# Count matrix of a graph: source one-hots of four columns in one vector operation, read against a row of numbers in PSUM

## The chip, the cores and the metric

The kernel runs on one core of one Trainium2 chip. The metric is the device time of one execution in microseconds (us), lower is better. A core has five engines that run their own instruction streams and meet at semaphores: PE (TensorE, matmuls; its weight loads are shown as PEld), DVE (VectorE), ACT (ScalarE), POOL (GpSimd) and SP (SyncE). Here POOL issues the indirect DMAs (gathers), and SP hands out buffers.

## What is computed

Four graph layers run one after the other on 6250 nodes of 128 features, with 106250 edges `src -> dst` and a 128-wide attribute per edge:

```python
x = layernorm(x + L0(x, src, dst))            # mean over in-neighbours
x = layernorm(x + L1(x, edge_attr, src, dst)) # H[head]@Wa + E@Wb, summed both ways over all edges
x = layernorm(x + L2(x, src, dst))            # two attention convolutions
x = layernorm(x + L3(x, src, dst))            # four mean aggregations, top k between them
```

The kernel turns `segment_sum(x[src], dst)` into dense matmuls with a count matrix `A[src, dst]` (how many edges lead from src to dst). Layer 1 also needs, per source node, the sum of the attributes of its edges. The change lies in the part that makes `A` and these sums.

## The kernel before, in words

Nodes are padded to NP = 6272 in NT = 49 tiles of P = 128. Part a sorts the edges by source into a list `listed` of COLS = 896 columns by 128 partitions; each entry has the edge's number, its destination and its source. Part b, which the change touches, loads the list as `entry`, and turns the sources and destinations into f32 (`key_id`, `key_dst`) and the sources into int16 as well (`key_src`).

**The matrix.** For each of 49 source tiles ("lines") and each of 7 windows of WIDE = 896 destinations there is a cell. A cell is a loop (`cell`, once on PE, once on DVE) whose turns take four columns of the list each. In a turn DVE makes for each of the four columns a one-hot of the source within the tile, 128 wide (L1009: compare the int16 row `iota` with the key of the partition), and a one-hot of the destination in the window, 896 wide (L1011). PE multiplies them (L823, two matmuls of 448 columns for each list column, eight a turn) into one of three PSUM buffers of two banks (`ps_cell`, banks 0 to 5). ACT copies a full buffer to `line` (L890), clears it (L880) and writes each line to `adjacency` in HBM. The one-hots stand in `hot`, a ring of two turns, each in two halves of two columns: `s_hot` tells PE that a half is written, `s_hot_free` tells DVE that PE has read one. Before each half DVE waits for the same half of the turn before last.

**The sums.** POOL gathers attribute rows of the list, eight columns to a unit and UNITS = 112 units, one indirect DMA for each column (L804), into `row_ring`, which holds four units. SP goes through the units in order: it waits until PE has summed unit u (L779, `s_sum`, a `hold` whose line is L69), gives its place free (L780, `s_unit_free`), and then waits for the four semaphores of the next unit of that place (L771) before it tells PE of it (L772, `s_rows`) and turns to unit u + 1. PE makes the sums in 81 steps of two (`two`, L832 to L844): each takes two pairs (tile, unit), for each of them eight f32 matmuls (L841) of the source one-hots `is_src` with the rows, into `ps_row`, banks 6 and 7. DVE adds a sum to `edges_out` (`add`, L1031) and makes the `is_src` of the step after next (`hot_of`, L1024, 128 x 1024 f32 out of two int16 tables in SBUF).

**The order** is written out by hand and the same on PE and DVE. PE: `two(i)`, cells 4 to 6 of line s, `two(i + 1)`, cells 0 to 3 of line s + 1. DVE: cells 4 to 6 of line s, `turned_over(i)`, cells 0 to 3 of line s + 1, `turned_over(i + 1)`. Each sixth line has no step of two (`TURN`). `hold` (L67 to L69) is a wait with an increment of a semaphore that nobody reads. `bc` is a broadcast by stride 0.

```python
for half in range(2):                                             # DVE, cell(), L1005
    hold(dve, s_hot_free, turn * 2 + (half + 1), s_held_dve)
    for j in range(2): ...                                        # L1009, L1011 for column 2 * half + j
for h in range(2):                                                # DVE, turned_over(), L1036
    add(i, h, pair[h]); hot_of(parity, h, later[h])
```

## Time and profile before

| what | value |
|---|---|
| median of 3 runs (lowest, highest) | 8150.13 us (8149.39, 8155.3) |
| the profiled execution, its span | 8157.6 us, 8155.7 us |
| PE, DVE, ACT, POOL busy over the span | 73%, 53%, 27%, 43% |
| part b, first to last matmul of the matrix | 1276 to 2803 us of the span |

The profiled execution is 7.5 us above the median of the runs; its span leaves out 1.9 us around the first and the last instruction. The profile gives for each group of instructions the line, the engine, how often it ran, the busy time, the mean of one, and the idle time of the engine before it with what ended that idle time. Such a wait is put down to the instruction whose semaphore came last. "issue" is idle time that no semaphore ended: the engine's own sequencer was still at loop, register and wait instructions, which are not counted as busy.

### The profile page before, as it was taken

The numbers are of one execution on the slowest core, as the hardware profiler recorded it, in microseconds if no ns is written. First come the engines' busy times: TensorE is split into PE (matmuls) and PEld (weight loads), VectorE is DVE, ScalarE is ACT, GpSimd is POOL, SyncE is SP. The second block draws the span as 40 slices with busy tenths as digits, with TensorE's granted clock in tenths as the row PEclk, the third lists the DMA queues.
The fourth block names the chain that finished last, engine by engine and source line by source line (L and its number), as shares of the span: only waits on it lengthen the run. The fifth ranks groups of instructions, "written<-read, shape, count | busy, mean of one in ns | idle before, by whom it ended". The sixth has DMA issues, their size and how long they took to land. (4 is left out here: it accounts for less than half of the span.)

```text
span 8155.7 us, 149095 instructions
## 1 busy us (share of the span) xinstructions
PE 5989.6 (73%) x38791; PEld 4139.6 (51%) x38792; DVE 4345.4 (53%) x11705; ACT 2230.5 (27%) x4994; POOL 3467.9 (43%) x3568
## 2 busy tenths in 40 slices
PE   0366625666666599999976777767777769996899
PEld 0255523334443255555546766757666635553555
DVE  9677737667776412222227777767777730103311
ACT  1011203434443300100004555535555500000200
POOL 4777766666665100000007777747777600000400
PEclk9987768999999899999988999989999989997999
DMA  0122212222223356777752222212222246663566
GB/s 18 43 71 69 71 38 79 91 98 96 92 96 95 79 169 171 180 188 179 191 125 57 54 55 56 54 48 54 55 55 55 47 129 188 191 198 113 146 195 178
DMA packets 835186, 849.24 MB, mean 104 GB/s; under 512 B 417947, under 2 KB 779130, under 8 KB 828347
## 3 DMA queue, kind: packets, MB, share of 16 engines
q1 hardware_dynamic: 710381, 560.82, 25.2%
q0 software_dynamic: 115904, 201.65, 10.9%
q10 hardware_dynamic: 8464, 81.36, 2.5%
q8 instruction: 222, 3.64, 0.2%
q14 instruction: 215, 1.76, 0.1%
HBM read 665.89 MB, written 97.31 MB: 94 GB/s over the span
## 5 line engine op out<-in xcount | busy, mean ns | idle before, releaser
L1954 POOL DMA_INDIRECT d_row_ring<-table_att,src_at x1664 | 1579.2, 949 | 639.0 <-issue 486.4
L2576 PE MATMUL psum<-e_a_ring,e_parts 128*128 128x448 bf16 x6174 | 1184.8, 353 | 75.9 <-DVE e_parts L2690 75.9
L804 POOL DMA_INDIRECT b_row_ring<-edge_attr,b_entry x896 | 902.4, 1007 | 565.3 <-SPq L780 325.2
L823 PE MATMUL psum<-b_hot 128*128 x2872 | 660.9, 367 | 462.4 <-DVE b_hot L1011 276.1
L363 POOL DMA_INDIRECT listed<-a_record,a_slot_no x832 | 811.8, 976 | 338.8 <-issue 271.9
L2576 PEld LDWEIGHTS psum<-e_a_ring,e_parts 128*128 128x128 bf16 x6174 | 605.1, 98 | 632.4 <-issue 81.0
L1363 PE MATMUL psum<-c_a_ring,c_parts 128*128 128x448 bf16 x4116 | 812.8, 356 | 45.4 <-DMA c_a_ring<-adjacency 40.7
L1979 PE MATMUL psum<-edges_out,edges_in 128*128 128x120 f32 x4896 | 678.2, 297 | 160.3 <-ACT edges_in L2045 159.3
L1979 PEld LDWEIGHTS psum<-edges_out,edges_in 128*128 128x128 f32 x4896 | 628.5, 208 | 205.7 <-issue 205.7
L823 PEld LDWEIGHTS psum<-b_hot 128*128 x2872 | 282.9, 98 | 820.7 <-issue 719.1
L1011 DVE TENSOR_SCALAR b_hot<-b_iota,b_key_dst 128x896 int16 x1436 | 690.1, 481 | 4.9 <-issue 4.6
L1995 PE MATMUL psum<-edges_out,edges_in 128*128 128x132 f32 x4896 | 651.5, 288 | 16.7 <-DVE edges_out L2217 15.9
L1009 DVE TENSOR_SCALAR b_hot<-b_iota,b_key_id (+1 forms) x1436 | 386.9, 269 | 450.3 <-PE psum L823 388.0
L1277 POOL DMA_DIRECT2D table_att<-c_h_row x21 | 15.7, 746 | 1431.6 <-DVEq L1701 1431.6
L1995 PEld LDWEIGHTS psum<-edges_out,edges_in 128*128 128x128 f32 x4896 | 598.0, 197 | 38.7 <-DVE edges_out L2217 23.7
L1363 PEld LDWEIGHTS psum<-c_a_ring,c_parts 128*128 128x128 bf16 x4116 | 404.4, 99 | 418.0 <-DMA c_a_ring<-adjacency 50.6
L890 ACT CAST b_line<-psum 128x896 f32 x343 | 310.4, 905 | 905.4 <-PE psum L823 871.9
L841 PE MATMUL psum<-b_row_ring,b_is_src 128*128 x2592 | 348.8, 295 | 218.7 <-SPq L772 143.4
L405 PE MATMUL psum<-a_later 128*128 x2432 | 418.5, 342 | 55.4 <-ACT a_later L448 55.0
L841 PEld LDWEIGHTS psum<-b_row_ring,b_is_src 128*128 128x128 f32 x2592 | 326.8, 206 | 257.8 <-issue 257.6
L405 PEld LDWEIGHTS psum<-a_later 128*128 128x128 f32 x2432 | 392.1, 251 | 128.2 <-issue 127.1
L2167 DVE TENSOR_TENSOR edges_in<-psum,edges_out 128x1024 bf16<-128x1024 f32 x306 | 374.7, 1224 | 106.3 <-issue 60.7
(477 smaller groups left out, 8043.1 us busy)
## 6 DMA issues: line engine op xcount, KB each, us to landing
e_a_ring<-adjacency SPq DMA_DIRECT2D x1029, 224.0 KB, 2.8
c_a_ring<-adjacency SPq DMA_DIRECT2D x686, 224.0 KB, 2.9
adjacency<-b_line ACTq DMA_DIRECT2D x49, 1568.0 KB
a_later<-edge_attr SPq DMA_DIRECT2D x103, 512.0 KB
d_row_ring<-table_att,src_at POOLq DMA_INDIRECT x1664
b_row_ring<-edge_attr,b_entry POOLq DMA_INDIRECT x896
listed<-a_record,a_slot_no POOLq DMA_INDIRECT x832
e_a_left<-adjacency_left SPq DMA_DIRECT2D x28, 224.0 KB, 3.3
```

Of the source, the lines that this page charges most:

```text
L363: pool.indirect_dma_start(out=listed, out_offset=bass.IndirectOffsetOnAxis(ap=slot_no[:, c:c + 1], axis=0), in_=record[:, c, :], in_offset ...
L405: mm = nc.tensor.matmul(ps_in[h], is_dst[:, h, c, :], row_ring[:, unit, c, :].rearrange("p a f -> p (a f)"), start=(c == 0), stop=(c == G ...
L804: pool.indirect_dma_start(out=row_ring[:, u % 4, g, 0:D], out_offset=None, in_=a["edge_attr_128"], in_offset=bass.IndirectOffsetOnAxis(ap= ...
L823: mm = nc.tensor.matmul(ps[:, v, :], four[:, half, j, 0:P], four[:, half, j, P + v * WIN:P + (v + 1) * WIN], start=False, stop=True, skip_ ...
L841: mm = nc.tensor.matmul(ps_row[h], is_src[:, parity, h, c, :], row_ring[:, bass.ds(unit & 3, 1), c, :].rearrange("p a f -> p (a f)"), star ...
L1009: V.tensor_scalar(four[:, half, j, 0:P], iota[:, bass.ds(tile * P, P)], ids[:, c:c + 1], None, ALU.is_equal)
L1011: last = V.tensor_scalar(four[:, half, j, P:], iota[:, window], ends_at[:, c:c + 1], None, ALU.is_equal)
L1363: mm = nc.tensor.matmul(psum[:, b + v, 0:WIN], parts[:, piece, tile, :], rows[:, v * WIN:(v + 1) * WIN], start=(s == 0 and piece == 0), st ...
L1954: pool.indirect_dma_start(out=row_ring[:, u % 4, g, :], out_offset=None, in_=table_att[layer], in_offset=bass.IndirectOffsetOnAxis(ap=src_ ...
L1979: mm = nc.tensor.matmul(psum[:, 3 + h, c * SLOTS:(c + AGAIN) * SLOTS], is_dst[:, h, c, :], bc(ranked[:, h, c, :], 1, [P, AGAIN, SLOTS]), s ...
L1995: mm = nc.tensor.matmul(ps_out, is_dst[:, h, c, :], weighted[:, c, :], start=(c == 0), stop=(c == G - 1))
L2576: mm = nc.tensor.matmul(psum[:, 2 * (turn % 2) + v, 0:WIN], (few_parts if d == 2 else parts)[:, piece, s, :], a_ring[:, (FIRST[turn] + s) ...
```

## The change

- `hot`'s four source one-hots of a turn are made by one DVE operation on 128 x 4 x 128 elements in place of four on 128 x 128: (key - first node of the tile) == position, with `key_id` broadcast along the 128 positions, the tile's first node as a scalar per partition out of the new table `tile_at` (made by one more iota on POOL), and the positions 0 to 127 out of `ps_iota`, a row of 128 f32 in PSUM bank 7, written once.
- `is_src` is made by the same kind of operation on 128 x 8 x 128, in place of a comparison of two int16 tables. `key_src` and the operation that fills it go.
- DVE waits once a turn, for both halves of the turn before last. `s_hot` is still told twice a turn, after the destinations of columns 0 and 1, and of 2 and 3.
- Both sums of a step lie in bank 6. PE therefore waits for both adds of the step before at the head of `two`, and DVE waits for both sums before its first add; `turned_over` makes both adds first and then both one-hots.

```diff
--- before.py
+++ after.py
@@ -132,7 +132,6 @@
         columns = sb("columns", [P, NT])
         tables = sb("tables", [P, 2 * COLS + COLS // 2 + P * QJ + UNITS + 1])
         column_key = tables[:, 0:COLS]
-        key_src = tables[:, 2 * COLS:2 * COLS + COLS // 2].bitcast(I16)
         out_pairs = tables[:, 2 * COLS + COLS // 2:2 * COLS + COLS // 2 + P * QJ].bitcast(I32)
         out_end = tables[:, 2 * COLS + COLS // 2 + P * QJ:].bitcast(I32)
         rank_peak = sb("rank_peak", [P, 1], I32)
@@ -680,6 +679,7 @@
             key_dst = sbb("key_dst", [P, COLS])
             reach = sbb("reach", [P, 2, COLS])
             hit = sbb("hit", [P, COLS])
+            tile_at = sbb("tile_at", [P, NT + 1])
             cell_no = sbb("cell_no", [P, CI])
             cell_f = sbb("cell_f", [P, 4, CI])
             cell_i = sbb("cell_i", [P, 2, CI], I32)
@@ -722,7 +722,8 @@
             s_left_out = bsem("s_left_out")
 
             ps_cell = [psum[:, 2 * k:2 * k + 2, 0:WIN] for k in range(3)]
-            ps_row = [psum[:, 6 + k, 0:D + 1] for k in range(2)]
+            ps_row = [psum[:, 6, h * (D + 1):(h + 1) * (D + 1)] for h in range(2)]
+            ps_iota = psum[:, 7, 0:P]
             buffer_of = [w % 3 for w in range(NWIDE)]
             last_use = [max(v for v in range(w - NWIDE, w) if buffer_of[v % NWIDE] == buffer_of[w]) for w in range(NWIDE)]
 
@@ -783,6 +784,7 @@
             @blk.gpsimd
             def _(pool):
                 nc.gpsimd.iota(iota[:], [[1, NP + P]], base=0, channel_multiplier=0)
+                nc.gpsimd.iota(tile_at[:], [[P, NT + 1]], base=0, channel_multiplier=0, allow_small_or_imprecise_dtypes=True)
                 nc.gpsimd.iota(cell_no[:], [[1, CI]], base=0, channel_multiplier=CI, allow_small_or_imprecise_dtypes=True)
                 nc.gpsimd.iota(cell_real[:], [[1, CI]], base=0, channel_multiplier=CI)
                 nc.gpsimd.iota(count_up[:, 0, :], [[-1, COLS]], base=COLS, channel_multiplier=0,
@@ -833,10 +835,10 @@
                         cell(ps_cell[buffer_of[w]], n, at0)
 
                 def two(i, parity, pair):
+                    pe.wait_ge(s_added, i * 2 + 2)
                     for h, (_, unit) in enumerate(pair):
                         hold(pe, s_rows, unit + 1, s_held_pe)
                         pe.wait_ge(s_is_src, i * 2 + (h + 1))
-                        pe.wait_ge(s_added, i * 2 + (h + 1))
                         for c in range(G):
                             mm = nc.tensor.matmul(ps_row[h], is_src[:, parity, h, c, :],
                                                   row_ring[:, bass.ds(unit & 3, 1), c, :].rearrange("p a f -> p (a f)"),
@@ -919,7 +921,6 @@
                 V = nc.vector
                 dve.wait_ge(s_entry, 16)
                 st.by(V.tensor_copy(key_id[:], entry[:, :, 2]))
-                st.by(V.tensor_copy(key_src, entry[:, :, 2]))
                 st.by(V.tensor_copy(key_dst[:], entry[:, :, 1]))
                 st.settle(dve)
                 st.by(V.tensor_copy(reach[:, 0, :], key_dst[:]))
@@ -990,6 +991,8 @@
                 st.by(V.tensor_tensor(cell_row[0:1, 1, :], cell_row[0:1, 1, :], cell_row[0:1, 0, :], ALU.bitwise_or))
                 st.settle(dve)
                 dve.wait_ge(s_table, 1)
+                st.by(V.tensor_copy(ps_iota, iota[:, 0:P]))
+                st.settle(dve)
                 dve.sem_inc(s_table, 1)
                 dve.sem_inc(s_hot_free, HOT)
                 dve.sem_inc(s_added, 2)
@@ -999,16 +1002,15 @@
                     with dve.Fori(0, n) as g:
                         k = nc.s_assert_within(dve.snap(k0 + g * 4), 0, COLS - 4,
                                                skip_runtime_bounds_check_because="k0 is at most COLS - 4 n")
-                        ids, ends_at = key_id[:, bass.ds(k, 4)], key_dst[:, bass.ds(k, 4)]
+                        ends_at = key_dst[:, bass.ds(k, 4)]
                         turn = dve.snap(at0 + g)
-                        four = hot[:, bass.ds(turn & 1, 1), :, :, :].rearrange("p a h j f -> p (a h) j f")
+                        four = hot[:, bass.ds(turn & 1, 1), :, :, :].rearrange("p a h j f -> p (a h j) f")
+                        hold(dve, s_hot_free, turn * 2 + 2, s_held_dve)
+                        V.scalar_tensor_tensor(four[:, :, 0:P], bc(key_id[:, bass.ds(k, 4)], 2, [P, 4, P]),
+                                               tile_at[:, bass.ds(tile, 1)], bc(ps_iota, 1, [P, 4, P]), ALU.subtract, ALU.is_equal)
                         for half in range(2):
-                            hold(dve, s_hot_free, turn * 2 + (half + 1), s_held_dve)
-                            for j in range(2):
-                                c = 2 * half + j
-                                V.tensor_scalar(four[:, half, j, 0:P], iota[:, bass.ds(tile * P, P)],
-                                                ids[:, c:c + 1], None, ALU.is_equal)
-                                last = V.tensor_scalar(four[:, half, j, P:], iota[:, window],
+                            for c in (2 * half, 2 * half + 1):
+                                last = V.tensor_scalar(four[:, c, P:], iota[:, window],
                                                        ends_at[:, c:c + 1], None, ALU.is_equal)
                             last.then_inc(s_hot, 1)
 
@@ -1021,12 +1023,13 @@
 
                 def hot_of(parity, h, code):
                     tile, unit = code
-                    V.tensor_tensor(is_src[:, parity, h, :, :], bc(key_src[:, bass.ds(unit * G, G)], 2, [P, G, P]),
-                                    bc(iota[:, bass.ds(tile * P, P)], 1, [P, G, P]), ALU.is_equal).then_inc(s_is_src, 1)
+                    V.scalar_tensor_tensor(is_src[:, parity, h, :, :], bc(key_id[:, bass.ds(unit * G, G)], 2, [P, G, P]),
+                                           tile_at[:, bass.ds(tile, 1)], bc(ps_iota, 1, [P, G, P]), ALU.subtract, ALU.is_equal
+                                           ).then_inc(s_is_src, 1)
 
                 def add(i, h, code):
                     at = bass.ds(code[0], 1)
-                    dve.wait_ge(s_sum, i * 2 + (h + 1))
+                    dve.wait_ge(s_sum, i * 2 + 2)
                     hold(dve, s_added, i * 2 + (h + 2), s_held_dve)
                     V.tensor_tensor(edges_out[:, at, :].rearrange("p a f -> p (a f)"),
                                     edges_out[:, at, :].rearrange("p a f -> p (a f)"), ps_row[h], ALU.add
@@ -1035,6 +1038,7 @@
                 def turned_over(i, parity, pair, later):
                     for h in range(2):
                         add(i, h, pair[h])
+                    for h in range(2):
                         hot_of(parity, h, later[h])
 
                 for i in range(2):
```

In DVE's loop of a cell (L1009, now L1009, the sources; L1011, now L1013, the destinations; ISA, REGISTER_ALU and the like are the sequencer's own). Before:

```order
L1009 ISA
L1009 TENSOR_SCALAR b_hot<-b_iota,b_key_id 128x128
L1011 ISA
L1011 TENSOR_SCALAR b_hot<-b_iota,b_key_dst 128x896
L67 REGISTER_ALU
L1009 ISA [waits b_s_hot_free]
L1009 TENSOR_SCALAR b_hot<-b_iota,b_key_id 128x128
L1011 ISA
L1011 TENSOR_SCALAR b_hot<-b_iota,b_key_dst 128x896
```

Now:

```order
L1009 REGISTER_ALU [waits b_s_hot_free]
L1009 ISA
L1009 REGISTER_ALU
L1009 ISA
L1009 SCALAR_TENSOR_TENSOR b_hot<-b_key_id,b_tile_at,psum 128x4x128
L1013 ISA
L1013 TENSOR_SCALAR b_hot<-b_iota,b_key_dst 128x896
```

A turn had eight DVE operations in alternation and a second wait in its middle; it now has one operation on the sources, then the four on the destinations, and the wait stands ahead of all five.

In DVE's `turned_over`, the first pair of a step (L1031, now L1034: the add; L1024, now L1026: the one-hots of the sources). Before:

```order
L67 REGISTER_ALU [waits b_s_sum]
L1031 REGISTER_ALU [waits b_s_added]
L1031 REGISTER_ALU
L1031 ISA
L1031 TENSOR_TENSOR edges_out<-edges_out,psum 128x129
L1024 REGISTER_ALU
L1024 ISA
L1024 REGISTER_ALU
L1024 ISA
L1024 TENSOR_TENSOR b_is_src<-tables,b_iota 128x1024
```

Now:

```order
L1034 TENSOR_TENSOR edges_out<-edges_out,psum 128x129
L67 REGISTER_ALU [waits b_s_sum]
L1034 REGISTER_ALU [waits b_s_added]
L1034 REGISTER_ALU
L1034 ISA
L1034 TENSOR_TENSOR edges_out<-edges_out,psum 128x129
L1026 REGISTER_ALU
L1026 ISA
L1026 REGISTER_ALU
L1026 ISA
L1026 SCALAR_TENSOR_TENSOR b_is_src<-b_key_id,b_tile_at,psum 128x1024
```

The second add moved ahead of the first one-hots.

On PE, the head of `two` (L838 and L841 before, L838 to L843 now). Before:

```order
L67 REGISTER_ALU
L67 ISA
L838 ISA [waits b_s_rows]
L841 REGISTER_ALU [waits b_s_added,b_s_is_src]
L841 ISA
L841 MATMUL psum<-b_row_ring,b_is_src 128x129
```

Now:

```order
L838 ISA
L67 REGISTER_ALU [waits b_s_added]
L67 ISA
L841 REGISTER_ALU [waits b_s_rows]
L843 REGISTER_ALU [waits b_s_is_src]
L843 ISA
L843 MATMUL psum<-b_row_ring,b_is_src 128x129
```

The wait for the adds moved ahead of the wait for the rows, and is made once for both pairs.

## Rows read from the trace of the kernel before

**Rows 1.** Groups of instructions by line, stretch 1276 to 2803 us (columns as first line)

```profile
line engine op names shapes xcount | busy us, mean ns | idle before us <-releasers
L804 POOL DMA_INDIRECT b_row_ring<-edge_attr,b_entry x867 | 865.5, 998 | 556.5 <-SPq L780 325.2 <-issue 231.3
L823 PE MATMUL psum<-b_hot 128*128 x2872 | 660.9, 367 | 462.4 <-DVE b_hot L1011 276.1 <-issue 164.7 <-ACT b_line L890 12.3
L841 PE MATMUL psum<-b_row_ring,b_is_src 128*128 x2592 | 348.8, 295 | 218.7 <-SPq L772 143.4 <-issue 60.1 <-DVE b_is_src L1024 11.1
L1024 DVE TENSOR_TENSOR b_is_src<-tables,b_iota 128x1024 f32 x160 | 195.5, 1222 | 8.6 <-issue 4.9
```

**Rows 2.** Waits, 1276 to 2803 us: who, for whom, us, times, longest us

```profile
DVE b_hot L1009 <- PE psum L823: 388.0, 161, 19.0
```

**Rows 3.** Waits of SP's queue, 1276 to 2803 us

```profile
SPq L771 <- DMA b_row_ring<-edge_attr,b_entry: 1352.4, 109, 18.5
SPq L69 <- PE psum L841: 24.6, 4, 7.8
```

**Rows 4.** Timeline, DVE and PE, 2035 to 2043 us: start us, us, engine, line

```profile
2035.01 1.74 PE L823 MATMUL psum<-b_hot 128*128 x8 [0.97 <-issue]
...
2037.05 0.25 DVE L1009 TENSOR_SCALAR b_hot<-b_iota,b_key_id  x1 [0.77 <-PE psum L823]
2037.22 0.45 DVE L1011 TENSOR_SCALAR b_hot<-b_iota,b_key_dst 128x896 int16 x1
2037.58 0.25 DVE L1009 TENSOR_SCALAR b_hot<-b_iota,b_key_id  x1
2037.68 1.82 PE L823 MATMUL psum<-b_hot 128*128 x8 [0.94 <-issue]
...
2040.01 0.25 DVE L1009 TENSOR_SCALAR b_hot<-b_iota,b_key_id  x1 [0.77 <-PE psum L823]
...
2040.47 1.77 PE L823 MATMUL psum<-b_hot 128*128 x8 [0.97 <-issue]
```

**Rows 5.** Timeline of PE, 1808 to 1834 us, a stretch of lines without a step of two

```profile
1811.57 1.75 PE L823 MATMUL psum<-b_hot 128*128 x8 [0.96 <-DVE b_hot L1011]
1816.66 8.04 PE L823 MATMUL psum<-b_hot 128*128 x24 [3.35 <-DVE b_hot L1011]
```

**Rows 6.** Timeline, a `turned_over` of DVE and the gathers of POOL under it

```profile
2023.97 0.94 POOL L804 DMA_INDIRECT b_row_ring<-edge_attr,b_entry  x1 [0.30 <-issue]
...
2024.32 0.28 DVE L1031 TENSOR_TENSOR edges_out<-edges_out,psum 128x129 f32 x1
2024.65 1.23 DVE L1024 TENSOR_TENSOR b_is_src<-tables,b_iota 128x1024 f32 x1
...
2025.22 1.47 POOL L804 DMA_INDIRECT b_row_ring<-edge_attr,b_entry  x1 [0.30 <-issue]
...
2027.13 0.25 DVE L1009 TENSOR_SCALAR b_hot<-b_iota,b_key_id  x1
```

**Rows 7.** Timeline of POOL, first and last of 46 long gathers under L1024

```profile
1325.20 1.83 POOL L804 DMA_INDIRECT b_row_ring<-edge_attr,b_entry  x1 [2.10 <-SPq L780]
...
2636.80 1.48 POOL L804 DMA_INDIRECT b_row_ring<-edge_attr,b_entry  x1 [6.19 <-SPq L780]
```

**Rows 8.** Instructions on tiles and lines: duration ns min/median/max, first and last start us

```profile
L804 POOL DMA_INDIRECT b_row_ring<-edge_attr,b_entry x896: 938/944/2454, 1229.5 to 2696.1; - x180
...
L2167 DVE TENSOR_TENSOR edges_in<-psum,edges_out x306: 1224/1224/1226, 4299.5 to 6505.0; 128x1024 bf16<-128x1024 f32 x153
...
L2217 DVE TENSOR_TENSOR edges_out<-d_row_ring,psum x306: 1247/1254/1256, 4318.2 to 6521.2; 128x1056 f32<-128x1056 f32 x153
```

**Rows 9.** The page's groups: the gathers of the attention layer

```profile
L1954 POOL DMA_INDIRECT d_row_ring<-table_att,src_at x1664 | 1579.2, 949 | 639.0 <-issue 486.4
```

**Rows 10.** Durations of two operations of the new kind (columns as rows 8)

```profile
L950 DVE SCALAR_TENSOR_TENSOR b_hit<-b_reach,b_cell_no,b_line x8: 1152/1152/1152, 1237.7 to 1253.9; 128x896 f32<-128x896 f32 x8
...
L2703 DVE SCALAR_TENSOR_TENSOR e_y<-psum,col_w_deg,e_r_b_s x98: 340/343/352, 6674.9 to 7459.2; 128x128 f32<-128x128 f32 x98
```

**Rows 11.** Timeline, the start of part b

```profile
1208.75 0.55 POOL L786 IOTA b_cell_no<- 128x4 f32 x1
...
1263.62 0.41 DVE L981 CAST b_hit<-b_cell_row 1x512 f32<-1x512 int32 x1 [4.93 <-DMA b_cell_row<-cell_rows]
```

## The prediction

> **What bounds the kernel now.** Only part b changes, 1527 us of the 8155.7 us span, so the question is what those 1527 us wait for. I read first the groups of that stretch, to see which engine is full. None is: the matmuls of the matrix and of the sums take 661 + 349 us of PE [rows 1]. So I read what PE's idle time ends with, and then the timeline of single turns.
>
> PE's turn. In a stretch with nothing but cells, PE starts a turn at 2035.01, 2037.68 and 2040.47 us, every 2.7 us; 1.8 us of it are the eight matmuls, and 0.94 to 0.97 us are idle with "issue" behind them, the loop's own registers [rows 4]. There are 2872 / 8 = 359 turns: 359 x 2.7 = 969 us. The 276 us that the groups put down to DVE are for the most part this same 0.95 us, and once, before the first turn, the start of the part. A step of two sums has 2592 / 81 = 32 matmul records, 349 / 81 = 4.3 us, and (218.7 - 143.4) / 81 = 0.9 us of idle time of its own [rows 1]: 81 x 5.2 = 421 us. That makes 1390 us of work that PE's instruction stream needs whatever the others do. The rest is one wait: 143.4 us for SP L772, the attribute rows [rows 1]. 1390 + 143 = 1533, against 1527.
>
> The row stream. SP spent 1352.4 us waiting for gathered rows, and 24.6 us, four times, waiting for PE [rows 3]. It frees a place only after the unit before has landed, so POOL never has more than one unit to fetch: eight gathers of 998 ns with 0.3 us between them, then 325.2 / 108 = 3.0 us until the next place is free [rows 1]. It is a serial chain over the whole part, nearly never held up by PE, and PE waits on it 143 us. **So the rows bound part b first, PE's own stream second; DVE is third:** it waits 388 us for PE to free one-hots [rows 2].
>
> **Part by part.**
>
> 1. *Four source one-hots in one operation.* Old: from L1009's start to L1011's is 0.17 us, from L1011's to the next L1009 0.36 us [rows 4]; a turn is 4 x 0.53 = 2.1 us, plus 0.77 us of idle time before the next turn, 2.96 us from 2037.05 to 2040.01. New operation, from its kind [rows 10]: 1152 ns for 896 elements and 343 for 128 give 1.053 ns an element and 208 ns fixed, so 512 elements last 747 ns; less the 0.08 us by which the next operation starts before the end (0.25 long, next after 0.17) that is 0.67 us, against 4 x 0.17 = 0.68. DVE's data time stays. What falls is its instruction stream: three operations with their register instruction and one wait fewer a turn. The turn can become anything from 2.1 us (the 0.77 all hidden) to 2.96 (nothing); I take 2.3, since five instructions of 0.67 and 0.36 us give the sequencer time that eight of 0.26 on average do not. By itself it earns nothing, because DVE is not the bound; see 4.
>
> 2. *One wait a turn, for both halves.* From PE's freeing to the first half ready was 0.77 + 0.17 + 0.36 + 0.17 + 0.45 = 1.9 us and becomes 0.77 + 0.67 + 0.36 + 0.45 = 2.25 us. `hot` holds two turns, so PE works 2.7 us on the other one meanwhile. Cost nothing; the cover is PE's turn, 0.45 us of it are left. Behind the wait stand this turn's five operations and, after a line's part, the adds, for which nobody is in haste, as PE needs them a step later.
>
> 3. *`is_src` out of one SBUF table and PSUM.* The operation gets longer, 208 + 1024 x 1.053 = 1286 ns against 1222: 162 x 0.06 = 10 us of DVE, hidden by its 388 us of waiting. What it does to POOL is the main term. A gather lasts 944 ns in the median [rows 8] but 998 in the mean [rows 1]: 867 x 54 = 47 us too long. Under L1024 a gather took 1.47 us, just before it 0.94 [rows 6]. 46 gathers of over 1.23 us overlap an L1024, the first and the last are shown [rows 7], together 32 us over the median, and all gathers that overlap one have 36 us of the 47. L1024 reads two SBUF tables. Where DVE instead reads one SBUF tensor and PSUM, in the attention layer, L2167 and L2217 run 306 x 2.5 = 760 us [rows 8] beside 1664 gathers whose mean is 949 [rows 9]. So the 36 us should go. Bounds: 0, if the new operation stops gathers as the old did, and 47. They are taken off a serial chain; PE's 143 us of row waits are there to be shortened by them. About a tenth of the units are fetched while it is PE that is late (SP's waits, three of them inside the part [rows 3]), so -33 us.
> The Trainium skill says otherwise here ("SBUF — State Buffer", Who interferes with whom): vector operations with two SBUF inputs disturb only GpSimd instructions that read SBUF, a `tensor_tensor` was seen not to stall a gather's descriptors, and it is `tensor_scalar` in its two-port modes that does. The trace has it the other way round, 1.47 us under L1024 against 0.94 under L1009 and L1011. By the page the sum would lose nearly all of this term; that is rival B.
>
> 4. *A faster DVE turn where DVE does set the pace.* On lines without a step of two, PE does seven and more cells in a row and DVE's 2.96 us are longer than PE's 2.7. There PE's idle time before a turn is 3.35 us instead of 0.96 [rows 5], 2.4 us too long, once in each of the eight blocks of six lines: 19 us. After most of them PE runs into a wait for rows anyway, which takes it back. Three of SP's waits for PE follow such a stretch, and after the last one no rows are waited for: 4 x 2.4 = -9 us. Bounds 0 and -19.
>
> 5. *Order of adds and the waits for them.* PE waits 11.1 us before L841 for L1024 [rows 1], which I read as the second add standing behind it. Now both adds come first. The same cells lie between as before, so no wait is added; what goes is mostly followed by a wait for rows. 0 (bounds -11, 0). DVE's wait for both sums: PE made them three cells earlier. 0.
>
> 6. *The start.* One more small iota on POOL, 0.55 us by its nearest row; the copy to PSUM, 0.41 by a copy of 512 [rows 11]; four longer `is_src`, 0.24; the first half 0.34 later (2.). The copy to `key_src` goes, beside POOL's iotas: nothing. +1.4 us.
>
> Sum: -33 - 9 + 1.4 = -41 us. The profiled execution, 8157.6 us, would become 8117; from the median of the runs, 7.5 us lower, 8150.1 - 41 = **8109 us**.
>
> **The rivals.** A difference under 0.2% (16 us) can't be told from none.
>
> A, the forecast: gathers freed of L1024. With the bounds of 3, 4 and 5: from -47 - 19 + 1 = -65 (8085) to -24 + 1 (8127) where a third of the gathers' 36 us stays and term 4 earns nothing.
>
> B, *the gathers stay as slow as they are*. Then only the share of the four small L1009 a turn goes. Outside L1024 the excess is 47 - 36 = 11 us, and L1009 has 0.17 of every 0.53 us: -3.5. With 4 and 6: -3.5 - 9 + 1.4 = -11, 8139 us, no difference. For it speaks the skill's rule above; against it rows 6 and 9.
>
> C, *slower: DVE becomes the bound*. If the new operation takes two cycles an element, it needs 0.53 us more, a turn is 2.96 + 0.53 = 3.5 us if the idle 0.77 us also stay, and a `turned_over`, 2.8 us now (2024.32 to 2027.13 [rows 6]), takes 2 x 1.07 more: 359 x 3.5 + 81 x 4.95 = 1657 us, 130 more than the 1527: 8280 us. The point from which it decides is a turn of (1527 - 401) / 359 = 3.1 us, 0.18 above today's. Answer time would be 2.8 us, over PE's 2.7. Against it stands row L950, two f32 SBUF sources and 1152 ns for 896 elements. The skill's "Vector Engine (DVE) Microarchitecture Reference", Points that are easy to get wrong, says that this shape with two non-bf16 SBUF sources has half the throughput; L950 doesn't show it, and here one source is in PSUM.
>
> D, more than forecast: terms 3, 4 and 5 all at their far bounds and PE's steps shorter besides, -47 - 19 - 11 + 1 = -76: below 8085.
>
> **How the numbers follow.** A 0.72, B 0.17, C 0.05, D 0.06. Faster: A and D, 0.78. Same: B, 0.17. Slower: C, 0.05. The range leaves out C and D and takes in B's price with a few us for the spread of the runs: 8085 to 8145; A's own range is 8085 to 8127.
>
> **What would show it.** The mean of the gathers near 955 ns (B: 990 and more); the `is_src` operation near 1290 ns and the new `hot` one near 750 (C: 1280); PE's wait for SP about 105 us instead of 143; DVE's idle time before its turns longer, its turn 2.3 us where it is not held; no 3.35 us before PE's turns. The forecast is wrong if gathers get faster and PE's wait for rows does not fall, for then the rows were not the chain that I take them for, and wrong in its second term if PE still stands before single turns for DVE, which would say that the answer time of 2. is longer than reckoned.

## The result and the profile after

The changed kernel takes 8168.2 us (median of 14 runs, 8159.7 to 8181.6) against 8150.9 (14 runs of the kernel before on the same chip; one of them took 20795 us and is left out of the ratio): ratio 1.0022, 95% interval 1.0015 to 1.0029, **slower by 17 us**. The forecast was 8109, 41 us faster. In two more comparisons the changed kernel was slower by 13.2 and 17.6 us; on average 16.

The groups of part b of the changed kernel (columns as in [rows 1]; L806 are the gathers, L825 and L843 PE's matmuls of the matrix and of the sums, L1009 the new operation for four source one-hots, L1013 the destinations, L1026 `is_src`, L1034 the adds):

```profile
L806 POOL DMA_INDIRECT b_row_ring<-edge_attr,b_entry x864 | 865.2, 1001 | 560.4 <-SPq L781 329.9 <-issue 230.4
L825 PE MATMUL psum<-b_hot 128*128 x2872 | 666.9, 372 | 452.9 <-DVE b_hot L1013 369.3 <-issue 75.4 <-ACT b_line L892 7.0
L1013 DVE TENSOR_SCALAR b_hot<-b_iota,b_key_dst 128x896 int16 x1435 | 561.2, 454 | 0.0
L843 PE MATMUL psum<-b_row_ring,b_is_src 128*128 x2592 | 353.5, 298 | 221.9 <-SPq L773 146.3 <-DVE b_is_src L1026 45.3 <-issue 29.9
L1009 DVE SCALAR_TENSOR_TENSOR b_hot<-b_key_id,b_tile_at,psum 128x512 f32 x358 | 266.8, 745 | 457.1 <-PE psum L825 387.1 <-issue 69.6
L1026 DVE SCALAR_TENSOR_TENSOR b_is_src<-b_key_id,b_tile_at,psum 128x1024 f32<-128x1024 f32 x160 | 197.8, 1278 | 11.1
L1034 DVE TENSOR_TENSOR edges_out<-edges_out,psum 128x129 f32 x162 | 46.3, 286 | 31.2 <-DVE edges_out L1034 30.8 <-issue 0.4
```

Against [rows 1]: the new operations last what was reckoned, 745 and 1278 ns. The gathers did not get faster: 1001 ns against 998, and PE waits 146.3 us for rows against 143.4 (138.2 and 145.8 in two more profiles of the changed kernel, 137.9 in a second one of the kernel before). PE's other idle time before the sums looks as if it had moved to `is_src` (45.3 against 11.1), but less the waits for rows it is 75.6 us against 75.3: only the last of several near ends has changed.

SP's waits say the same as [rows 3]: rows bound it, PE hardly ever.

```profile
SPq L772 <- DMA b_row_ring<-edge_attr,b_entry: 1355.5, 109, 18.7
SPq L69 <- PE psum L843: 28.6, 4, 12.0
```

Part b, from the first to the last matmul of the matrix, takes 1530.3, 1524.3 and 1524.1 us in three profiles, and 1527.1 and 1524.1 in two of the kernel before: it has hardly changed. Most of what can be found of the 16 us is in code that the change doesn't touch. In the attention layer, the first L2167 of [rows 8] and the last stand 2205.5 us apart; in the changed kernel, where it is L2171, 2214.9:

```profile
L2171 DVE TENSOR_TENSOR edges_in<-psum,edges_out x306: 1224/1224/1226, 4301.3 to 6516.2; 128x1024 bf16<-128x1024 f32 x153
```

So there are two questions: why did part b not gain the 42 us of terms 3 and 4, and why does the attention layer take longer?

### The profile page after: what moved, and what is told of

It reads as the page before. It is cut to its first block and busy times, and to the rows that moved or that the text cites. A ratio compares the mean times of both kernels' runs of the same rounds, so it can differ in the third digit from the quotient of the medians.

```text
span 8165.3 us, 145945 instructions
## 1 busy us (share of the span) xinstructions
PE 6006.6 (74%) x38753; PEld 4169.3 (51%) x38792; DVE 4308.0 (53%) x10628; ACT 2230.1 (27%) x4994; POOL 3467.2 (42%) x3569
## 5 line engine op out<-in xcount | busy, mean ns | idle before, releaser
L806 POOL DMA_INDIRECT b_row_ring<-edge_attr,b_entry x896 | 902.4, 1007 | 570.0 <-SPq L781 329.9
L825 PE MATMUL psum<-b_hot 128*128 x2872 | 666.9, 372 | 452.9 <-DVE b_hot L1013 369.3
L1983 PE MATMUL psum<-edges_out,edges_in 128*128 128x120 f32 x4896 | 698.2, 302 | 159.2 <-ACT edges_in L2049 158.1
L1983 PEld LDWEIGHTS psum<-edges_out,edges_in 128*128 128x128 f32 x4896 | 647.0, 213 | 204.8 <-issue 204.8
L825 PEld LDWEIGHTS psum<-b_hot 128*128 x2872 | 286.8, 100 | 811.4 <-issue 709.3
L1999 PEld LDWEIGHTS psum<-edges_out,edges_in 128*128 128x128 f32 x4896 | 605.3, 199 | 42.4 <-DVE edges_out L2221 29.5
L1013 DVE TENSOR_SCALAR b_hot<-b_iota,b_key_dst 128x896 int16 x1436 | 561.6, 454 | 0.0
L843 PE MATMUL psum<-b_row_ring,b_is_src 128*128 x2592 | 353.5, 298 | 221.9 <-SPq L773 146.3
L1009 DVE SCALAR_TENSOR_TENSOR b_hot<-b_key_id,b_tile_at,psum 128x512 f32 x359 | 267.6, 745 | 457.1 <-PE psum L825 387.1
L843 PEld LDWEIGHTS psum<-b_row_ring,b_is_src 128*128 128x128 f32 x2592 | 332.8, 210 | 259.3 <-issue 259.0
L2049 ACT CAST edges_in<-edges_in 128x1024 f32<-128x1024 bf16 x306 | 319.8, 1045 | 410.5 <-DVE edges_in L2171 363.0
```

The lines of the kernel that those rows point to most:

```text
L806: pool.indirect_dma_start(out=row_ring[:, u % 4, g, 0:D], out_offset=None, in_=a["edge_attr_128"], in_offset=bass.IndirectOffsetOnAxis(ap= ...
L825: mm = nc.tensor.matmul(ps[:, v, :], four[:, half, j, 0:P], four[:, half, j, P + v * WIN:P + (v + 1) * WIN], start=False, stop=True, skip_ ...
L843: mm = nc.tensor.matmul(ps_row[h], is_src[:, parity, h, c, :], row_ring[:, bass.ds(unit & 3, 1), c, :].rearrange("p a f -> p (a f)"), star ...
L1013: last = V.tensor_scalar(four[:, c, P:], iota[:, window], ends_at[:, c:c + 1], None, ALU.is_equal)
L1983: mm = nc.tensor.matmul(psum[:, 3 + h, c * SLOTS:(c + AGAIN) * SLOTS], is_dst[:, h, c, :], bc(ranked[:, h, c, :], 1, [P, AGAIN, SLOTS]), s ...
L1999: mm = nc.tensor.matmul(ps_out, is_dst[:, h, c, :], weighted[:, c, :], start=(c == 0), stop=(c == G - 1))
```

## Experiments on part b

The ratios are against the kernel before in the same comparison. The *excess* of a profile is, over the 864 to 868 gathers of part b, the sum of what each lasted above 944 ns. "Expected" texts are as they stood before the run; their "count part" is part b.

**The changed kernel again.**

> The changed kernel again, for a second profiled execution beside the first, because its 9.6 us over the kernel before stood for 3 us in part b (1527.1 to 1530.3 us from the first to the last matmul of the matrix) and for 9.6 us in the attention layer, whose code the change does not touch (2260.8 to 2270.3 us, with 349 us of it at the lower granted clock against 292). Theory W (part b's own waits: gathers and DVE's answers): part b again 1530 or longer, the attention layer anywhere between 2260 and 2270 by chance of that execution. Theory K (the change shifts what follows, by its place in time or in memory): the attention layer again near 2270 with about 350 us at the lower clock. Time about 8168 us in both.

8169.0 us, ratio 1.0017 (1.0008 to 1.0026), part b 1524.3, excess 48 us: slower by as much as the first time. Neither theory came whole. Part b was back at 1524, against W; the attention layer stayed longer than before, 2211.2 us, but the lower granted clock did not come with it as K had it: between the first and the last L2171 TensorE had the lower of its two clock levels for 256 us here, 307 in the first profile and 250 in the kernel before.

**Only `is_src` changed: the matrix's one-hots made as before.**

```diff
-                        hold(dve, s_hot_free, turn * 2 + 2, s_held_dve)
-                        V.scalar_tensor_tensor(four[:, :, 0:P], bc(key_id[:, bass.ds(k, 4)], 2, [P, 4, P]),
-                                               tile_at[:, bass.ds(tile, 1)], bc(ps_iota, 1, [P, 4, P]), ALU.subtract, ALU.is_equal)
+                            hold(dve, s_hot_free, turn * 2 + (half + 1), s_held_dve)
+                            for j in range(2):
+                                c = 2 * half + j
+                                V.tensor_scalar(four[:, half, j, 0:P], iota[:, bass.ds(tile * P, P)],
+                                                ids[:, c:c + 1], None, ALU.is_equal)
```

> Only the source one-hots of the sums are made with the row in PSUM (and both sums in bank 6, which frees bank 7); the matrix's one-hots alternate as before, in halves. Theory 1 (a gather is held up by L1024's two SBUF tables, and in the changed kernel by four wide tensor_scalar in a row, which alternation with narrow ones does not do): gathers' mean about 957 ns instead of 998, PE's wait for SP about 110 us instead of 143, part b about 1495 us, total 8115 to 8125 us. Theory 2 (the gathers' excess of some 47 us is there whatever DVE does): mean about 1000 ns, total 8150 us.

**Only the bank, the waits and the order**, in the kernel before:

```diff
-            ps_row = [psum[:, 6 + k, 0:D + 1] for k in range(2)]
+            ps_row = [psum[:, 6, h * (D + 1):(h + 1) * (D + 1)] for h in range(2)]
...
+                    pe.wait_ge(s_added, i * 2 + 2)
-                        pe.wait_ge(s_added, i * 2 + (h + 1))
...
-                    dve.wait_ge(s_sum, i * 2 + (h + 1))
+                    dve.wait_ge(s_sum, i * 2 + 2)
...
+                    for h in range(2):
```

> Only both sums in bank 6, with the wait for both adds at the head of two, the wait for both sums and the adds first; all one-hots as before. Theory 1: no term, 8145 to 8155 us. Rival (the second add, which now stands waiting for the first, holds DVE's instruction stream 0.8 us a step and makes PE wait): part b longer by 5 to 15 us, 8155 to 8165 us.

**Pairs:** the changed kernel with an operation for each two columns, after its own half's wait and ahead of its two destinations.

```diff
-                        hold(dve, s_hot_free, turn * 2 + 2, s_held_dve)
-                        V.scalar_tensor_tensor(four[:, :, 0:P], bc(key_id[:, bass.ds(k, 4)], 2, [P, 4, P]),
-                                               tile_at[:, bass.ds(tile, 1)], bc(ps_iota, 1, [P, 4, P]), ALU.subtract, ALU.is_equal)
+                            hold(dve, s_hot_free, turn * 2 + (half + 1), s_held_dve)
+                            V.scalar_tensor_tensor(four[:, 2 * half:2 * half + 2, 0:P],
...
```

> The changed kernel with two operations of two columns in place of one of four, each after the wait for its own half and ahead of its two destination one-hots, so that wide tensor_scalar stand in runs of two, not four, and DVE answers PE by halves again. Theory 1: gathers' excess between: mean 965 to 980 ns, part b about 1510 us, 8130 to 8145 us. If it is the wait for the whole turn that costs: PE's waits for DVE back to the level of before, the gathers as in the changed kernel, 8150 us. If neither counts: 8168 us as the changed kernel.

| kernel | median | ratio (95%) | part b | excess |
|---|---|---|---|---|
| before, twice | 8150.9 | | 1527.1, 1524.1 | 47, 38 |
| changed, three times | 8168.2 | 1.0022 (1.0015-1.0029) | 1530.3, 1524.3, 1524.1 | 49, 48, 54 |
| before, beside the next three | 8155.8 | | | |
| only `is_src` | 8144.5 | 0.9985 (0.9976-0.9994) | 1499.7 | 10 |
| only bank, waits, order | 8165.5 | 1.0016 (1.0007-1.0025) | 1526.0 | 41 |
| pairs | 8169.5 | 1.0020 (1.0011-1.0029) | 1526.0 | 55 |

With `is_src` alone, the gathers and part b do what term 3 said; the total, 11 us less than the kernel before beside it, missed the 8115 to 8125 expected. The groups of that kernel:

```profile
L806 POOL DMA_INDIRECT b_row_ring<-edge_attr,b_entry x865 | 826.5, 955 | 569.3 <-SPq L781 338.6 <-issue 230.7
L843 PE MATMUL psum<-b_row_ring,b_is_src 128*128 x2592 | 349.2, 296 | 199.2 <-SPq L773 121.8 <-DVE b_is_src L1027 55.9 <-issue 21.4
```

955 ns a gather (forecast: 955), 22 us less waiting for rows, part b 24 to 27 us shorter. So the way in which the matrix's one-hots are made gives the gain back. Sorting each gather's excess by the DVE operations that ran during it shows how: in the kernel before, 36 of the 47 us lie in gathers that overlap L1024, and 11 in the 511 that overlap only the narrow and wide one-hots in turn, 21 ns each (28 and 10 of 38 in its second profile). In the changed kernel none lie under L1009 or L1026 alone; 27 lie in 161 gathers that overlap only L1013, 168 ns each, and 16 in 255 that overlap L1013 and L1009. The wide L1013 was there before, but never two in a row. With pairs, two in a row, I had expected 965 to 980 ns a gather and a part b of 1510 us; the mean is 1008 and the excess no smaller (55), so two suffice.

The kernel with only the bank, the waits and the order has the old part b, 1526.0, and is 10 us slower all the same (6 to 20 by its interval), where I had expected either no cost or 5 to 15 us inside part b: these edits cost nothing there, and what they cost lies elsewhere.

**Both at once:** the changed kernel with `is_src` made as before, out of two int16 tables.

```diff
-                    V.scalar_tensor_tensor(is_src[:, parity, h, :, :], bc(key_id[:, bass.ds(unit * G, G)], 2, [P, G, P]),
-                                           tile_at[:, bass.ds(tile, 1)], bc(ps_iota, 1, [P, G, P]), ALU.subtract, ALU.is_equal
-                                           ).then_inc(s_is_src, 1)
+                    V.tensor_tensor(is_src[:, parity, h, :, :], bc(key_src[:, bass.ds(unit * G, G)], 2, [P, G, P]),
+                                    bc(iota[:, bass.ds(tile * P, P)], 1, [P, G, P]), ALU.is_equal).then_inc(s_is_src, 1)
```

> The changed kernel with the source one-hots of the sums made as before (two int16 tables in SBUF): only the four-column operation, the one wait a turn and the bank. Theory 1 (both hold gathers up: L1024, and four wide tensor_scalar in a row): the two add up, gathers' mean 1030 to 1050 ns, PE's wait for SP 170 us or more, part b 1545 to 1565 us, total 8180 to 8200 us. Theory 2 (the excess is some 47 us whatever DVE does; the source-only run was then an exception): mean 1000 ns, 8168 us as the changed kernel.

8194.4 us, ratio 1.0058 (1.0046 to 1.0071), part b 1544.7, and the largest excess of all, 86 us: some 37 under the old `is_src` and 49 elsewhere, near the 36 that lay under it before and the changed kernel's 49.

```profile
L807 POOL DMA_INDIRECT b_row_ring<-edge_attr,b_entry x866 | 904.5, 1044 | 537.9 <-SPq L782 306.8 <-issue 231.1
```

**The turn of adds and source one-hots:** only `is_src` changed, with add, one-hots, add, one-hots as in the kernel before.

```diff
                     for h in range(2):
                         add(i, h, pair[h])
-                    for h in range(2):
                         hot_of(parity, h, later[h])
```

> The source-only kernel with the order add, one-hots, add, one-hots as before the change, both waits for two and the one bank kept. If it is the second add waiting for the first that holds DVE's stream (80 times 0.8 us in the changed kernel's trace) and makes PE wait for DVE (24 us there, 16 before the change): PE's waits for DVE back to 16 us, part b 1490 to 1495 us, 8135 to 8140 us. If the order does not count: 8144 us as the source-only kernel. If PE now waits at the head of two for the late second add: longer, 8150 us.

8142.0 us, 0.9990 (0.9981 to 0.9999), part b 1499.4. DVE's 31 us of waits of the second add for the first are gone, and PE's wait for `is_src` fell from 55.9 to 12.5 us, but no time went with them: term 5's zero was right.

**The chain of rows.** SP frees a place before it waits for the landing of the unit before; the rest as in the kernel before.

```diff
-                for u in range(4):
+                for u in range(3):
...
-                        arrived(u, i + 1)
+                        arrived((u + 3) % 4, i if u == 0 else i + 1)
+                arrived(3, UNITS // 4 - 1)
```

> The kernel before again, for a second profiled execution. In its first one part b took 1527.1 us and the attention layer 2260.8; in the five others so far the attention layer, the same code, took 2266.5 to 2278.6. If that layer varies by chance of the execution: anything from 2260 to 2280 here. If it is the changed memory or order of part b that lengthens it: 2261 again.

> The kernel before, with one thing changed that the change under study does not touch: SP frees a place of the row ring before it waits for the landing of the unit before, so that two units are on their way. Theory 1 (the rows are one serial chain of gather, landing and freeing, and PE waits on it 143 us): POOL's wait for SP falls from 3.0 us a unit to little, PE's wait for rows to under 30 us, part b to about 1400 us, total 8025 to 8045 us. Rival (PE's waits come from the gathers' own rate or from HBM): part b loses under 30 us, above 8125 us.

The kernel before took 8151.0 again (part b 1524.1). This one took 8021.4 us, 0.9847 (0.9834 to 0.9861), part b 1395.7:

```profile
L842 PE MATMUL psum<-b_row_ring,b_is_src 128*128 x2592 | 324.6, 284 | 97.1 <-issue 71.3 <-SPq L772 18.2 <-DVE b_is_src L1025 7.3
```

143.4 us of waiting for rows became 18.2: the reading of the row stream as the chain that bounds part b, and of PE as second at some 1390 us, is confirmed.

## Experiments on the attention layer

Its length (first to last L2167; the expected texts count to the layer's last matmul, some 55 us more) was 2204.3 to 2208.1 us in the three profiles of kernels with the old waits, and 2211.2 to 2223.4 in all six kernels with PE's one wait for both adds, whether or not anything else was changed. In the compiled programs everything behind part b stands 22 instructions earlier on PE in those six, and on DVE 9 to 409 earlier. The first experiment gives PE the 22 back, where it waits 10 us for DVE anyway:

```diff
+                for _ in range(22):
+                    pe.sem_inc(s_sum, 1)
                 pe.wait_ge(s_left_n, 1)
```

> The changed kernel with 22 extra instructions on PE (increments of a semaphore that nobody waits for any more) behind the count part's matrix, where PE waits 10 us for DVE. Counted in the compiled programs, everything of PE behind the count part stands 22 instructions earlier in the changed kernel than in the one before, since PE waits for the adds once where it waited twice; with the 22 it stands where it stood. Theory P (the attention layer, whose code the change does not touch, is 6 to 18 us longer in all seven kernels with the one wait because PE's instructions lie elsewhere): attention layer back from 2266-2270 us to 2260-2264, total about 8161 against 8168. Rival Q (what the layer takes depends on the state that the count part leaves, on the clock or on the DVE's program): attention layer stays at 2266-2270, total stays at 8168.

> The same 22 instructions in the kernel with the matrix one-hots of before, the source one-hots from PSUM and the two in turn (8142 us, attention layer 2275.5). Theory P: attention layer 2260-2264, total about 8130 (8142 less 12), count part unchanged at 1499 us. Rival Q: 2266-2278 and 8142.

> The kernel before with 234 such instructions, which moves PE's later code to where the changed kernel has it, 256 instructions further on. Theory P, if what matters is the place within a block of 256 instructions or of any power of two below: attention layer 2266-2275 and total about 8159 (8150 plus 9, and up to some us for the instructions themselves). If P holds but with another period, anything from 2260 to 2278. Rival Q: 2260-2264 and 8150.

Then DVE's 409 as well, by a loop that was meant to make no turn, and DVE's alone:

```diff
+                none = dve.value_load(cell_row[0:1, 2, 0:1], min_val=0, max_val=1)
+                with dve.Fori(0, none):
+                    for _ in range(402):
+                        dve.sem_inc(s_added, 1)
                 dve.wait_ge(s_reach_all, 2)
```

> The changed kernel a third time, beside p5_after_both on one chip: 8160 to 8169 us, attention layer 2266 to 2271, DVE's gap between the two register operations of the attention layer's row loop 9.3 us over 99 (2.9 in the kernel before).

> The changed kernel with PE's 22 extra instructions and, on DVE, a loop of no turns whose body is 402 instructions, so that all later code of both engines stands where it stands in the kernel before (counted in the compiled programs: PE 2175 and DVE 2553 instructions ahead of the layers' part, as before). Theory P2 (place of both engines' code): attention layer 2260 to 2264, DVE's gap back to 2.9 us over 99, total 8150 to 8157. Theory P (PE's alone): attention 2260 to 2271, DVE's gap 2.9, total as with the 22 alone, 8157. Rival Q (state left by the count part): attention 2266 to 2271 and 8160 to 8169.

> The changed kernel with DVE's later code where it stood before (a loop whose body is 402 instructions; it takes 39 us in p5_after_both) and PE's not. If PE's place is what the attention layer feels: 2266 to 2275 us in it, total less the loop's 39 us about 8162. If DVE's: 2259 to 2264 and about 8152.

> The changed kernel with PE's 22 extra instructions once more (2271 us and 8157 the first time). If PE's place decides: 2259 to 2264 in most executions, total 8150 to 8157. If both are needed or DVE's decides: again about 2271 and 8157 or more.

| kernel | instructions ahead of the layers, PE / DVE | attention layer | median less that of before |
|---|---|---|---|
| before, twice | 2175 / 2553 | 2205.5, 2204.3 | 0 |
| changed, three times | 2153 / 2144 | 2214.9, 2211.2, 2219.2 | +17.3, +13.2, +17.6 |
| changed, PE's back, twice | 2175 / 2144 | 2215.7, 2216.4 | +9.9, +15.8 |
| changed, DVE's back | 2153 / 2553 | 2215.1 | +50.6, of it the loop 39.2 |
| changed, both back | 2175 / 2553 | 2203.9 | +40.7, of it the loop 39.2 |
| `is_src` in turn | 2153 / 2544 | 2219.7 | -7.2 |
| the same, PE's back | 2175 / 2544 | 2204.4 | -14.0 |
| before, 234 more on PE | 2409 / 2553 | 2205.5 | +35.3, of it some 30 the instructions |

The loop did not come for nothing (whether it made a turn wasn't seen): DVE's gap where it stands is 42.14 us, 42.19 in the kernel with DVE's alone, against 2.95 in the changed kernel, and the difference is what is taken off.

```profile
2829.11 0.15 DVE L1075 TENSOR_SCALAR b_most<-b_most_all 128x1 f32<-128x1 f32 x1 [42.14 <-issue]
```

```profile
2787.19 0.15 DVE L1069 TENSOR_SCALAR b_most<-b_most_all 128x1 f32<-128x1 f32 x1 [2.95 <-issue]
```

These are the same row of the kernel with both back and of the changed one; and here is the layer with both back, and with DVE's alone:

```profile
L2177 DVE TENSOR_TENSOR edges_in<-psum,edges_out x306: 1224/1225/1226, 4328.0 to 6531.9; 128x1024 bf16<-128x1024 f32 x153
```

```profile
L2175 DVE TENSOR_TENSOR edges_in<-psum,edges_out x306: 1223/1224/1226, 4337.7 to 6552.8; 128x1024 bf16<-128x1024 f32 x153
```

The operation itself lasts the same 1224 ns everywhere; only the distances between them grow. A gap between two of DVE's register instructions in the row loop, 2.9 us in 99 times before and 9.3 in the changed kernel, is 2.9 again wherever DVE's code is back, but the layer is short only with PE's too. What part b leaves in memory is no cause, since the two kernels of these rows run the same part b. **The place of the later code is one:** with both engines' back the layer has its old length and the kernel is 1.5 us from the kernel before (the interval reaches 11 us to either side); with one of them the layer keeps its new length (2215 to 2216). That PE's place counts by itself where DVE's is near the old one, the pair with `is_src` in turn shows (2219.7 and 2204.4). Over all 20 profiles, the seven with PE at 2175 or 2409 and DVE at 2544 or 2553 have 2203.9 to 2208.2 us, the other thirteen 2211.2 to 2223.4. Theory P as first put, PE's place alone, fell with its profiles of 2215.7 and 2216.4; rival Q fell too, as far as it is about memory or DVE's program.

The granted clock is a rival that the padding does not exclude. Between the first and the last L2167, TensorE had the lower of its two levels for 229 to 270 us in the seven short layers and for 256 to 318 us in the other thirteen. It can't be the whole cause: where the two groups overlap, the layers of 267 and 270 us at the lower level took 2205.5 and 2208.2 us, those of 256, 257, 263 and 271 us took 2211.2 to 2215.7. Nor do whole executions follow it: the kernel before took 8151.6 us on average in 42 runs with a mean granted clock below 0.905 and 8149.9 in 53 above 0.915. How much of the layer's ten us is clock, and whether the place changes the clock, stays open.

What about a place costs the time stays open. The Trainium skill says that an engine's instruction memory is refilled in 16 KiB blocks ("Runtime: NRT & Kernel Launch", Terms) and that an instruction is 64 bytes wide ("Vector Engine (DVE) Microarchitecture Reference", Instruction fetch and dispatch), which by my estimate would make the place within 256 instructions the one that counts. The kernel with 234 more on PE has the changed kernel's place in that sense and the old layer length, which speaks against it for PE; where the loader really puts the code wasn't seen.

## The version that beats both

The changed kernel with the earlier freeing, and `is_src` in turn with it, without and with PE's 22 instructions:

> The changed kernel with the earlier freeing of a place (which took the kernel before to 8021 us, PE's waits for rows from 143 to 18 us, count part 1396 us). With the chain of rows gone, what the gathers lose to a run of four wide DVE operations no longer sets the time, and PE's waits for DVE do: expected count part 1396 to 1405 us, attention layer 2266-2270, total 8028 to 8040. If instead the contention of the gathers still set the pace, the count part would be 3 us and more behind and the gathers' waits on PE would stay above 40 us.

> The version made of what helped: the matrix one-hots of before (wide and narrow in turn, waited for by halves), the source one-hots by way of PSUM in turn with the adds, and the earlier freeing of a place. With the chain of rows gone the gathers' gain is hidden and PE's waits for DVE set the count part: 1388 to 1396 us, attention layer 2268 to 2276, total 8022 to 8035; if the gathers still mattered it would be 8000 or less.

> The same with PE's 22 extra instructions. Theory P: attention layer 2260 to 2264 and 5 to 12 us less than e8_best. Rival Q: no difference from it beyond 3 us.

| kernel | median | ratio (95%) | part b | attention layer |
|---|---|---|---|---|
| before, early freeing | 8021.4 | 0.9847 (0.9834-0.9861) | 1395.7 | 2208.1 |
| changed, early freeing | 8017.9 | 0.9848 (0.9834-0.9861) | 1385.9 | 2214.8 |
| `is_src` in turn, early freeing | 8012.9 | 0.9832 (0.9818-0.9845) | 1377.8 | 2211.9 |
| the same, PE's 22 | 8010.3 | 0.9826 (0.9813-0.984) | 1379.7 | 2208.2 |

The changed kernel and the one with `is_src` in turn were expected some 10 us later than they came (8028 and 8022 at the least), since part b gained more than I had put in; the 22 instructions gave 2.6 us and 4 in the layer, too little to tell P from Q by the medians. The change is worth 10 us in part b once the chain of rows is gone, though its gathers take 1018 ns (954 with `is_src` in turn): PE's idle time before the matrix's matmuls is 469.6 us with the change and 483.4 without. The attention layer takes 7 of them back, and the intervals of the two totals don't tell them apart. With only `is_src` changed part b gains 18, so the four-column operation loses 8 us there. The last two rows can't be told apart either; they are 135 and 138 us faster than the kernel before, nearly all of it by the freeing.

## Why the prediction was wrong

- **What bounds part b** (the row chain, then PE at some 1390 us, DVE third): right. Taking the chain away left 1395.7 us.
- **Term 1**, duration of the new operation 747 ns: 745. DVE's turn was put at 2.3 us; in the stretch of [rows 4] it is 2.77 (2035.63, 2038.39 and 2041.16 us in the rows below), against 2.96. Elsewhere turns do follow each other by 2.1 us (1510.72 and 1512.86 below); here 0.56 of idle time with "issue" behind it stands between them, which I had reckoned to be hidden.

```profile
2035.63 0.75 DVE L1009 SCALAR_TENSOR_TENSOR b_hot<-b_key_id,b_tile_at,psum 128x512 f32 x1 [1.36 <-PE psum L825]
2038.39 0.75 DVE L1009 SCALAR_TENSOR_TENSOR b_hot<-b_key_id,b_tile_at,psum 128x512 f32 x1 [0.56 <-issue]
2041.16 0.75 DVE L1009 SCALAR_TENSOR_TENSOR b_hot<-b_key_id,b_tile_at,psum 128x512 f32 x1 [0.57 <-issue]
```

- **Term 2**, one wait a turn costs nothing: no cost in part b's time was found, and pairs, which wait by halves, are no faster; but see the stops under term 4.
- **Term 3, -33 us, is the step that failed.** Its reason holds: `is_src` out of PSUM leaves the gathers alone, and alone it takes some 26 us off part b. What failed is the sum over the parts: I charged the old excess to L1024 and took L1011 for harmless, since gathers lasted 0.94 us under it. It was harmless only in turn with narrow operations, and term 1's edit took these away. The excess went from 47 and 38 us to 49, 48 and 54 instead of to nearly nothing, and the two edits together leave part b where it was (1524.1 to 1530.3 us against 1524.1 and 1527.1). Rival B, the gathers stay as slow, is what the part did, by another way than the one it named. The rule of the Trainium skill weighed there ("SBUF — State Buffer", Who interferes with whom) was half right: wide `tensor_scalar` operations do hold the gathers up, 168 ns each where only they run; but the `tensor_tensor` with two SBUF inputs does so too, 375 ns each in the 70 gathers that overlap only it and the adds (259 in 78 in the second profile).
- **Term 4, -9 us**, earned nothing, and its own sign of being wrong showed: PE still stands before single turns for DVE. In the stretch of [rows 5] the stops of 3.35 and, here, 3.21 us

```profile
1827.91 1.85 PE L823 MATMUL psum<-b_hot 128*128 x8 [3.21 <-DVE b_hot L1011]
```

  became 2.96 and 3.19:

```profile
1813.51 4.68 PE L825 MATMUL psum<-b_hot 128*128 x16 [2.96 <-DVE b_hot L1013]
1819.30 1.74 PE L825 MATMUL psum<-b_hot 128*128 x8 [1.11 <-DVE b_hot L1013]
1824.24 7.63 PE L825 MATMUL psum<-b_hot 128*128 x24 [3.19 <-DVE b_hot L1013]
```

  DVE's turn of 2.77 us is still longer than PE's 2.7, and at most 0.4 of the 2.4 us went. Over part b the stops became more: of those of 2.3 to 5 us that the profile puts down to L1011 (now L1013) there are ten in each of two profiles of the kernel before, and sixteen, two in each block, in each of three of the changed one (eleven with pairs). Nor do turns alone make them: in eight of the sixteen, and four of the ten before, DVE is at the adds and `is_src` while PE stands, as before 1813.51:

```profile
1808.14 0.28 DVE L1034 TENSOR_TENSOR edges_out<-edges_out,psum 128x129 f32 x1
1809.24 2.47 DVE L1026 SCALAR_TENSOR_TENSOR b_is_src<-b_key_id,b_tile_at,psum 128x1024 f32<-128x1024 f32 x2
1811.63 0.74 DVE L1009 SCALAR_TENSOR_TENSOR b_hot<-b_key_id,b_tile_at,psum 128x512 f32 x1
```

  These take 3.5 us between two turns, and term 4 did not price them. Why the stops became more was not tried. With the row chain gone, the changed kernel still has sixteen and a part b 8 us longer than the kernel with `is_src` in turn, which has eight.
- **Term 5**, 0, and **term 6**, +1.4: right; the first matmul of the matrix is 0.9 us later in the profile.
- **"Only part b changes"**, the first sentence, was the other mistake. The text of the later code is the same, its place isn't: about 15 of the 16 us, by the kernel with both places restored (+1.5). Of these the profiles show some 10 in the attention layer, a part of which may be the clock. The intervals of the medians reach 6 to 11 us to either side, so that number is rough, and in the same way the kernel with only `is_src` changed gained 11 us in the median where its part b is 27 shorter; where the rest of that went I can't say beyond the 6 us that its attention layer is longer.

The forecast said -41 and the runs +16: some 33 from term 3, 9 from term 4, and, roughly, 15 from the place of code that nobody had edited.

## What to carry to other kernels

Contention belongs to the order of operations, not to a kind alone: before several narrow operations between wide ones are merged into one, look at what other engine used the gaps, and try each edit by itself, since two that cancel look like one that does nothing. Ask of a stream with the highest wait whether its chain can be cut (here an order of two waits, 128 us) before polishing what runs beside it. And where an edit of a kernel of many instructions comes with under 0.2% more time in code behind it, try a padded version before you look for a reason in the edit.

## What the hardware did that was not expected

- Wide `tensor_scalar` (128 x 896, int16 in) back to back hold up a gather that overlaps only them by 168 ns on average; in turn with 128 x 128 ones by 21. Of the changed kernel's gathers, the one at 1548.03 stands under four in a row, the one at 1546.61 under the end of four, an L1009 and the start of the next four, and those at 1507.97 and 1509.21 under `is_src` from PSUM:

```profile
1507.67 2.47 DVE L1026 SCALAR_TENSOR_TENSOR b_is_src<-b_key_id,b_tile_at,psum 128x1024 f32<-128x1024 f32 x2
1507.97 0.94 POOL L806 DMA_INDIRECT b_row_ring<-edge_attr,b_entry  x1 [0.30 <-issue]
1509.21 0.94 POOL L806 DMA_INDIRECT b_row_ring<-edge_attr,b_entry  x1 [0.30 <-issue]
...
1510.72 0.75 DVE L1009 SCALAR_TENSOR_TENSOR b_hot<-b_key_id,b_tile_at,psum 128x512 f32 x1 [0.57 <-issue]
...
1512.86 0.75 DVE L1009 SCALAR_TENSOR_TENSOR b_hot<-b_key_id,b_tile_at,psum 128x512 f32 x1
...
1545.38 1.54 DVE L1013 TENSOR_SCALAR b_hot<-b_iota,b_key_dst 128x896 int16 x4
1546.61 1.12 POOL L806 DMA_INDIRECT b_row_ring<-edge_attr,b_entry  x1 [0.30 <-issue]
1546.86 0.75 DVE L1009 SCALAR_TENSOR_TENSOR b_hot<-b_key_id,b_tile_at,psum 128x512 f32 x1
1547.53 1.54 DVE L1013 TENSOR_SCALAR b_hot<-b_iota,b_key_dst 128x896 int16 x4
1548.03 1.15 POOL L806 DMA_INDIRECT b_row_ring<-edge_attr,b_entry  x1 [0.30 <-issue]
```

- The length of a loop nest of 306 rows went with where the code of two engines lies, by some 10 us in 2210, and both places count: 2203.9 to 2208.2 us in seven profiles with both near the old place, 2211.2 to 2223.4 in thirteen without. What makes it so is open.
- Increments of a semaphore are not free: 234 on PE took some 30 us more than the 10 us of idle time that they stood in (40.97 us of "issue" before the next matmul).
